# Feed-forward weights turned by VectorE in 32x32 blocks instead of by TensorE

## The reference, cut to what matters

```python
def _mx_dequant(t):                      # blocks of 32 along the last axis
    blocks = t.reshape(rows, feat // 32, 32)
    scales = jnp.maximum(jnp.max(jnp.abs(blocks), axis=-1) / 448.0, 1e-30)
    q = (blocks / scales[..., None]).astype(jnp.float8_e4m3fn).astype(jnp.float32)
    return (q * scales[..., None]).reshape(rows, feat)

x2d = layernorm(x)                                       # 1024 x 512
gate = _mx_dequant(x2d) @ _mx_dequant(gate_w).T          # gate_w, up_w: 2048 x 512
up   = _mx_dequant(x2d) @ _mx_dequant(up_w).T
h    = silu(gate) * up                                   # 1024 x 2048
x    = x + _mx_dequant(h) @ _mx_dequant(down_w).T        # down_w: 512 x 2048
```

## Time and profile before

| What | Before |
|---|---|
| Median of 3 runs | 1952.19 us (1952.12 to 1955.88) |
| Span of the profiled execution | 1951.1 us; the median of the runs is 1.1 us above it |
| PE busy | 1859.3 us, 95% |
| DVE busy | 1261.4 us, 65% |
| ACT busy | 698.1 us, 36% |
| POOL busy | 340.2 us, 17% |
| Mean granted TensorE clock | 0.985 |
| Weight transposes of the last stage (L2897, f_w) | 192 |
| First and last of them start | 1579.0 and 1877.6 us |

### The profile page before, as it was taken

The page is one execution under the profiler, slowest core; times in us unless marked ns, Lnnn a source line. Parts: engine busy times, 40 slices in busy tenths (PEclk is TensorE's granted clock), DMA queues, the critical chain, the costliest instruction groups (busy, mean ns, idle before and its releaser), DMA issues. The chain is left out here.

```text
span 1951.1 us, 24909 instructions
## 1 busy us (share of the span) xinstructions
PE 1859.3 (95%) x9496; PEld 1398.7 (72%) x9496; DVE 1261.4 (65%) x2133; ACT 698.1 (36%) x1123; POOL 340.2 (17%) x258
## 2 busy tenths in 40 slices
PE   7999999899999999999999999999989999999998
PEld 5777876444443578758888888888878875788886
DVE  5324755665761666686787687787762498866656
ACT  3302232345445478732342342333234331222211
POOL 0000010211200268711121111211210001212122
PEclk9999998999999899999999999999999999999999
DMA  6102222233321221132222213314212100110101
GB/s 217 44 0 71 87 71 55 50 74 74 93 50 46 85 66 66 44 123 88 77 78 101 97 58 111 105 39 133 76 35 76 65 25 19 65 44 24 42 1 44
DMA packets 69638, 132.58 MB, mean 68 GB/s; under 512 B 8960, under 2 KB 27392, under 8 KB 67984
## 3 DMA queue, kind: packets, MB, share of 16 engines
q1 hardware_dynamic: 69520, 130.99, 21.3%
HBM read 97.21 MB, written 14.75 MB: 57 GB/s over the span
## 5 line engine op out<-in xcount | busy, mean ns | idle before, releaser
L784 DVE TENSOR_REDUCE b_nm<-ps 128x1 f32<-128x1024 f32 x128 | 153.1, 1219 | 91.2 <-PE ps L772 91.2
L1270 ACT ACTIVATE b_pr<-ps 128x512 f32<-128x512 f32 x256 | 133.5, 603 | 135.6 <-PE ps L1182 135.4
L230 PE MATMUL ps<-d_x_high,d_w_high 128*128 128x512 f32 x384 | 154.6, 403 | 1.7 <-issue 1.7
L232 PE MATMUL ps<-d_x_high,d_w_low 128*128 128x512 f32 x384 | 150.0, 391 | 0.0
L231 PE MATMUL ps<-d_x_low,d_w_high 128*128 128x512 f32 x384 | 149.9, 390 | 0.0
L1194 PE MATMUL ps<-b_pr,b_VS 128*64 128x512 f32 x512 | 131.3, 637 | 0.0
L2229 POOL TENSOR_TENSOR d_sqsum<-d_sqsum,d_sq 128x512 f32<-128x512 f32 x32 | 45.4, 1422 | 468.4 <-ACT d_sq L2141 468.1
L1727 POOL TENSOR_TENSOR c_h<-c_h,c_w_row 128x512 f32<-128x512 f32 x64 | 105.7, 1657 | 50.4 <-DMA c_w_row<-w_rows 27.9
L1182 PEld LDWEIGHTS ps<-b_qS,b_kS 98*128 98x128 f32 x256 | 43.9, 193 | 78.5 <-issue 52.1
L1182 PE MATMUL ps<-b_qS,b_kS 98*128 98x512 f32 x256 | 93.1, 447 | 7.0 <-ACT b_pr L1270 3.5
L772 PE MATMUL ps<-b_kS,b_qS 96*128 96x512 f32 x256 | 82.6, 408 | 5.8 <-DVE b_nm L784 4.5
(11 more groups left out here) (439 smaller groups left out, 4971.0 us busy)
## 6 DMA issues: line engine op xcount, KB each, us to landing
b_kS<-b_k_parts SPq DMA_DIRECT2D x96, 128.0 KB, 2.3
f_rows<-d_fw SPq DMA_DIRECT2D x24, 512.0 KB, 3.8
f_w<-f_rows SPq DMA_DIRECT2D x12, 1024.0 KB, 4.8
c_w_row<-w_rows SPq DMA_DIRECT2D x16, 512.0 KB, 3.6
b_qS<-b_q_parts SPq DMA_DIRECT2D x96, 64.0 KB, 2.0
a_convT<-in_convT SPq DMA_DIRECT2D x4, 1024.0 KB, 12.8
d_w<-in_d_wq SPq DMA_DIRECT2D x16, 256.0 KB, 3.7
d_w<-in_d_wk SPq DMA_DIRECT2D x16, 256.0 KB, 2.8
```

The lines of the kernel that those rows point to most:

```text
L230: nc.tensor.matmul(out, lhsT[0], rhs[0], start=start, stop=False)
L232: return nc.tensor.matmul(out, lhsT[1], rhs[0], start=False, stop=stop)
L784: nc.vector.tensor_reduce(nm[:, g % 2, u:u + 1], c.ps[:, banks:banks + 2, :], AX.XY, ALU.max, negate=True).then_inc(job_read, 1)
L1270: nc.scalar.activation(pr[:, n % RING, :], c.ps[:, 4 + n % BANKS, :], ACT.Exp).then_inc(exp_done, 1)
```

## The change

The weight tiles are no longer turned by PE. DVE turns each in 32x32 blocks from `f_w` into one staging tile `wS` (128x512, a single buffer); ACT copies the staging tile as the high part; POOL subtracts to get the low part. DVE may turn the next tile only when POOL has done the low part of the one before.

Since DVE can only turn within a group of 32 partitions, the raw weights are loaded in another layout: each of the 48 tile loads becomes 4 DMAs, one for each group of 32 partitions, with runs of 128 features (512 bytes). With that the features come out in another order over the partitions, and the normalised x and h are written in the same order (`scale_by_blocks`, and `by_blocks` in the product of h).

```diff
-            sp.dma_start(fw[:, u % FSLOTS, i * BANK:(i + 1) * BANK], raw_rows(c, FR * u + i)).then_inc(in_f[u % FSLOTS], 16)
+            for b in range(P // MX):
+                sp.dma_start(fw[b * MX:(b + 1) * MX, u % FSLOTS, i * BANK:(i + 1) * BANK].rearrange("o (c f) -> o c f", f=P),
+                             raw_rows(c, FR * u + i, b)).then_inc(in_f[u % FSLOTS], 16)
...
+    def scale_by_blocks(self, dve, t):
+        nc.vector.tensor_scalar(by_blocks(c.xn[:, t, :]), in_order(c.x[:, t, :]), c.mv[:, t, 0:1], c.rstd[:, t:t + 1],
+                                ALU.subtract, ALU.mult).then_inc(self.normed, 1)
...
+    wS = c.at("f_wS", [P, KD, P], F32, 205.5)
...
-                    sp.wait_ge(turned, TURN_AT[("w", j - 2, KD - 1)] + 1)
+                    sp.wait_ge(w_turned, KD * (j - 1))
...
# GpSimd
+            def lows(units):
+                for i in units:
+                    pool.wait_ge(w_high_done, i + 1)
+                    high_, low_ = weight_parts(i)
+                    nc.gpsimd.tensor_tensor(low_, wS[:], high_.bitcast(F32), ALU.subtract).then_inc(w_low_done, 1)
+
+            lows(range(W_FIRST))
             for t in range(TT):
                 norm.root_pool(pool, t)
...
+            for s in range(STEPS + LAG):
+                early, middle, late = w_places(s) if s < STEPS else ([], [], [])
+                lows(early)
+                for u in ROUNDED_AT.get(s, []):
+                    products(XU + u)
+                lows(middle + late)
+                for u in SCALED_AT.get(s, []):
+                    ratios(XU + u)
...
# VectorE
+            def turn_weights(i):
+                dve.wait_ge(in_w[i // KD % 2], 16 * (i // KD // 2 + 1))
+                if i >= 1:
+                    dve.wait_ge(w_low_done, i)
+                nc.vector.transpose(wS[:].rearrange("p k (c o) -> p c k o", o=MX),
+                                    w[:, i // KD % 2, i % KD * DM:(i % KD + 1) * DM]
+                                    .rearrange("p (c k i) -> p c k i", k=KD, i=MX)).then_inc(w_turned, 1)
+
+            def weights_on(units, s):
+                for i in units:
+                    if i + 1 in w_turns(s):
+                        turn_weights(i + 1)
+
+            def weights_ahead(s):
+                if s < STEPS and w_turns(s):
+                    turn_weights(w_turns(s)[0])
...
             shift(NJ - 1)
+            turn_weights(0)
             for j, (b, m) in enumerate(JOBS):
...
-                low(TURNS[j])
+                if j + 1 < W_FIRST:
+                    turn_weights(j + 1)
...
-                for r in early:
-                    low(r)
+                weights_on(early, s)
                 for u in ROUNDED_AT.get(s, []):
                     unit_round(XU + u)
-                for r in middle:
-                    low(r)
+                weights_on(middle, s)
                 if s < STEPS:
...
-                    nc.vector.tensor_tensor(h[:, s % HR, :], c.ps[:, 4 + s % 2, :], silu[:, s % 2, :],
-                                            ALU.mult).then_inc(h_done, 1)
-                    for r in late:
-                        low(r)
+                    nc.vector.tensor_tensor(by_blocks(h[:, s % HR, :]), in_order(c.ps[:, 4 + s % 2, :]),
+                                            in_order(silu[:, s % 2, :]), ALU.mult).then_inc(h_done, 1)
+                    weights_on(late, s)
                     for u in SCALED_AT.get(s, []):
                         unit_scales(XU + u)
+                weights_ahead(s + 1)
...
# TensorE
-                turn(TURNS[j])
...
                     pe.wait_ge(low_done, TURN_AT[("x", t)] + 1)
-                    pe.wait_ge(low_done, TURN_AT[("w", 3 * n + 1, KD - 1)] + 1)
+                    pe.wait_ge(w_low_done, KD * (3 * n + 2))
                     up(s, 2 + s % 2, gT, silu_done, g_done)
-                    for r in middle:
-                        turn(r)
                     up(s, 4 + s % 2, uT, h_done, u_done)
-                    for r in late:
-                        turn(r)
...
# ScalarE
+            def high_turned(i):
+                act.wait_ge(w_turned, i + 1)
...
+                nc.scalar.activation(weight_parts(i)[0], wS[:], ACT.Copy).then_inc(w_high_done, 1)
...
-                high(TURNS[j])
+                high_turned(j)
...
-                    for r in early:
-                        high(r)
+                    for i in early:
+                        high_turned(i)
                     act.wait_ge(g_done, s + 1)
...
                     nc.scalar.activation(silu[:, s % 2, :], c.ps[:, 2 + s % 2, :], ACT.Silu).then_inc(silu_done, 1)
-                    for r in middle + late:
-                        high(r)
+                    for i in middle + late:
+                        high_turned(i)
```

More of the change, by code:

```diff
@@ L20, with raw_rows, by_blocks, in_order @@
 FJOBS = [(name, n) for n in range(4) for name in ("f_g", "f_u", "f_d")]
-def raw_rows(c, i):
+def raw_rows(c, i, b):
     name, n = FJOBS[i // KD]
-    rows = slice((i % KD) * P, (i % KD + 1) * P)
+    rows, cols = slice((i % KD) * P, (i % KD + 1) * P), slice(b * P, (b + 1) * P)
     if name == "f_d":
-        return c.dram[name][rows, n * BANK:(n + 1) * BANK]
-    return c.dram[name][n * BANK:(n + 1) * BANK, :][rows, :]
+        w = c.dram[name][:, n * BANK:(n + 1) * BANK]
+    else:
+        w = c.dram[name][n * BANK:(n + 1) * BANK, :]
+    return w[rows, cols].rearrange("(c o) f -> o c f", o=MX)
+def by_blocks(rows):
+    return rows.rearrange("p (k b i) -> p b k i", k=KD, i=MX)
+def in_order(rows):
+    return rows.rearrange("p (b k i) -> p b k i", k=KD, i=MX)
 class Core:
@@ L2634, in w_turns @@
         first = 0 if n == 0 else 2 * (t % 2)
-        return [("w", j, first + i) for i in range(count)] if 3 * n + 2 <= j < len(FJOBS) else []
+        return [KD * j + first + i for i in range(count)] if 3 * n + 2 <= j < len(FJOBS) else []
     def w_places(s):
@@ L2659, in mx_feed_forward @@
     FIRST = [("x", 0), ("x", 1)]
-    TURNS = [("w", j, r) for j in range(2) for r in range(KD)] + FIRST
+    TURNS = list(FIRST)
     for s in range(STEPS + LAG):
-        TURNS += x_turns(s) + h_turns(s) + (w_turns(s) if s < STEPS else [])
+        TURNS += x_turns(s) + h_turns(s)
     TURN_AT = {e: i for i, e in enumerate(TURNS)}
+    W_FIRST = 2 * KD
+    w_turned, w_high_done, w_low_done = (c.sem(f"f_{n}") for n in ("w_turned", "w_high_done", "w_low_done"))
     in_w = [c.sem(f"f_in_w{i}") for i in range(2)]
@@ L2712, in turn_parts, with weight_parts @@
         return [p_[:, e[1] % 2, :, :] for p_ in hF]
-    def bank_at(i):
-        return 4 + i % 2 if i < 2 * KD else i % 2
+    def weight_parts(i):
+        name, n = FJOBS[i // KD]
+        into = {"f_g": gT, "f_u": uT, "f_d": dT}[name]
+        return [p_[:, n % 2, :, i % KD * P:(i % KD + 1) * P] for p_ in into]
     def turn_bank(e):
-        return c.ps[:, bank_at(TURN_AT[e]), :].rearrange("p (k o) -> p k o", k=KD)
+        return c.ps[:, TURN_AT[e] % 2, :].rearrange("p (k o) -> p k o", k=KD)
     def e_tile(part, t):
@@ L2842, in _ @@
                 if t >= 1:
-                    norm.scale_dve(dve, t - 1)
+                    norm.scale_by_blocks(dve, t - 1)
                 if t == 2:
@@ L2896, in turn @@
                 for k in range(KD):
-                    last = nc.tensor.transpose(c.ps[:, bank_at(i), k * P:(k + 1) * P], turn_rows(e)[:, k * P:(k + 1) * P], c.ident[:])
+                    last = nc.tensor.transpose(c.ps[:, i % 2, k * P:(k + 1) * P], turn_rows(e)[:, k * P:(k + 1) * P], c.ident[:])
                 last.then_inc(turned, 1)
@@ L3013, in high @@
                 act.wait_ge(turned, TURN_AT[e] + 1)
-                if e[0] == "w" and e[2] == 0:
-                    name, n = FJOBS[e[1]]
+                if e[0] == "h" and e[1] >= 2:
+                    act.wait_ge(out_done, e[1] - 1)
+                nc.scalar.activation(turn_parts(e)[0], turn_bank(e), ACT.Copy).then_inc(high_done, 1)
+            def high_turned(i):
+                act.wait_ge(w_turned, i + 1)
+                if i % KD == 0:
+                    name, n = FJOBS[i // KD]
                     if name == "f_d" and n >= 2:
@@ L3020, in high @@
                         act.wait_ge(u_done, TT * (n - 1))
-                elif e[0] == "h" and e[1] >= 2:
-                    act.wait_ge(out_done, e[1] - 1)
-                nc.scalar.activation(turn_parts(e)[0], turn_bank(e), ACT.Copy).then_inc(high_done, 1)
+                nc.scalar.activation(weight_parts(i)[0], wS[:], ACT.Copy).then_inc(w_high_done, 1)
             def high_weights(i):
```

30 lines of the change are left out of this document (6 added, 24 removed).

## The result

The changed kernel takes 1960.15 us (median of 4 runs, 1958.47 to 1961.56), the kernel before beside it 1952.38 (4 runs, 1952.12 to 1955.88): ratio 1.0039, 95% interval 1.0027 to 1.0051. It is slower by 7.8 us, 0.4%. The profiled execution took 1959.69 us with a span of 1957.5, so 6.4 us more span than before.

What follows compares the result with a forecast made beforehand. PE was taken as the bound, except in the gate jobs and steps 0 to 8; 17.7 at step 8 + 1.6 clock - 12.3 for steps 10 to 27 = +7.0, span 1958.1, with 1.1 outside 1959.2 us; range 1951 to 1971.

Steps and rivals of the forecast that it cites:

- The turn on DVE: Every weight tile: one DVE turn takes 0.68 us, with bounds 0.42 and 1.22.
- The rivals with a cheap tile: Twelve tiles of steps 5 to 7: 1.80 us each gives 1948, chance 0.12; 2.23 each gives 1953, chance 0.12.
- Steps 10 to 27, -12.3: Later steps, PE the bound: 28 turns at 0.44 us removed gain 12.3 us; the 14 steps shrink to 8.65.
- The slack that I had worked out: Steps with two tiles: h's low part ends at 4.2 us, PE needs it at 5.9; slack 1.7, no wait.
- the fifth rival: Two-tile steps don't fit: a tile takes 3.7 us, no gain in steps 10 to 27, total 1983; chance 0.08.
- The chain of twelve, step 8 17.7 us late: Steps 5 to 8: twelve tiles 32.8 us plus 8.0 between them put step 8's gate product 17.7 us later.
- the 5.0 in step 6: Third tile of step 6: POOL's low part stands behind products, which wait for DVE's whole rounding; +5.0 us.
- The clock, +1.6: PE's restart in step 8 after its pause: a low granted clock costs 1.6 us, bounds 0 and 5.7.
- The gate jobs, -0.8: Gate jobs: 0.8 us gained, not 3.5, as the last numerators wait for DVE's products of z and gate.
- Linear attention, 0: Linear attention: 144 more DMAs on SP cost nothing, up to +9.6 us; the rival with that cost had chance 0.08.
- where I had 1.1: Time outside the span: 1.1 us, added to the forecast span of 1958.1.

Runs made afterwards that it cites:

- step 6 tiles first: Changed kernel with step 6's two middle tiles queued ahead of DVE's rounding and POOL's products: 1960.56 us, ratio to before 1.0044.
- PE kept busy: Changed kernel with 44 more PE products into an idle bank ahead of the wait of step 8: 1959.94 us, ratio to before 1.0038.
- the kernel with the loads alone: Kernel before with only the raw weight loads in the new layout, PE still turning the tiles: 1951.20 us, ratio to before 0.9993.
- the one with two staging tiles: Changed kernel with two staging tiles used in turn, all tiles still turned by DVE: 1947.03 us, ratio to before 0.9968.
- the kernel with PE on steps 5 and 6: Changed kernel with two staging tiles and PE turning the eight tiles of steps 5 and 6: 1944.89 us, ratio to before 0.9954.
- the last two experiments: Changed kernel with two staging tiles, PE turning the tiles of step 5 only (1943.02 us) or of steps 5 and 6 (1944.89 us).
- DVE's low parts: Changed kernel with the low parts of the first 20 tiles taken by DVE instead of POOL: 1957.44 us, ratio to before 1.0032.

## Why the prediction was right

Forecast 1959.2, measured 1960.15, by the mechanism forecast; that the two are so close is in part luck, as the end of this section shows. By the prediction's own steps:

- **The turn on DVE**: 0.68 taken, 0.698 measured. By the fixed term that the Trainium skill, VectorE: DVE Perf Modes, gives in its section on the TRN2 errata, my estimate had been 0.69; the trace agrees. With ACT's 0.63 and POOL's 1.28 and hand-overs a tile takes 2.82 (2.73 forecast). The Trainium skill, GPSIMD Engine Reference, section Performance versus the Vector engine, would have had the low part at 1.1 us (estimate); the measured 1.28 decides. The rivals with a cheap tile fall with it.
- **Steps 10 to 27, -12.3**: from the gate product of step 8 to the end TensorE's turns were worth 13.1 (252.9 against 239.8, two kernels with the chain out of the way). From the turn of h in step 10 to that in step 28 it is 12.5 (168.0 against 155.6). The other 0.6 lies behind the last turn of h, was not forecast, and its cause stays open. The slack that I had worked out held: no step of two tiles waits, and the fifth rival falls.
- **The chain of twelve, step 8 17.7 us late**: relative to the outputs 18.8 late (18.5 forecast). Its first turn came at 1674.31, 1.6 before 1675.9 as the outputs did; twelve tiles took 33.8 (32.8 forecast) and what stands between them 7.2 (8.0). PE stood 12.15 us ahead of step 6 and 13.44 ahead of step 8, where I had 12 and 16. My account of the 5.0 in step 6, though, had DVE's rounding in it only by way of POOL's order; the experiment that changed the order showed DVE's own work to hold the tiles up as long.
- **The clock, +1.6**: 2.3 (242.1 against 239.8), within its bounds.
- **The gate jobs, -0.8**: the step that was mis-sized, by its sign too. They took 2.3 us more: 0.6 for DVE's turn ahead of job 0, which came as forecast, and 1.7 from the first gF to the first sum of x, where I had 1.4 less. DVE's turn waited for POOL behind jobs 0, 3 and, which I had missed, 6. DVE and PE in order of time, and a window:

```profile
1604.51 7.94 PE L3016 MATMUL ps<-e_woT,e_gF 128*128 128x512 f32 x14 [0.78 <-DVE e_gF L2880]
...
1605.29 0.71 DVE L2801 STREAM_TRANSPOSE f_wS<-f_w 128x512 f32<-128x512 f32 x1 [0.81 <-POOL f_uT_low L2774]
...
1609.91 0.69 DVE L2885 TENSOR_TENSOR x<-ps,x 128x512 f32<-128x512 f32 x1 [2.62 <-PE ps L3016]
```

```profile
1604.00:1608.00 4.00, 3.49 (x5) 1.48 (x6) 2.45 (x4) 1.04 (x2) 2.44 (x2) 0.57 0.20 43
```

  PE had not waited for gF before; now it did four times, 3.1 us in all, and the granted clock fell to 0.57 behind the last of them. From the first output tile to its sum it took 5.4 us instead of 3.6. In two of the experiments with the same code (step 6 tiles first, PE kept busy) the clock did not fall there and the stretch was 30.7 and 30.6, with the same four waits of PE. So the waits alone use up what PE's turns gave, the turn ahead of job 0 adds its 0.6, and the clock adds 1.6 to 1.8.
- **Linear attention, 0**: shown by the kernel with the loads alone (535.6 us from the first to the last d_w_high in both, 535.8 after).
- **What the sum left out**: all that lies ahead of the gate jobs came 3.9 us earlier. 2.3 of it is there at the first d_w_high (831.5 before, 829.2 after), ahead of all that was changed; over the twelve profiled kernels this row lies between 828.1 and 831.8. The other 1.6 is at the end of the linear attention, where after is alone among the twelve (48.6 us from the last d_w_high to the last d_sq, the others 50.1 to 50.3). I take both for the spread of one execution. And 2.2 us lay outside the span after, where I had 1.1; over the experiments that part is 1.7 to 2.2, once 3.3, and what makes it up stays open.

So the errors of the sum (+3.1 in the gate jobs, +0.7 for the clock, +0.3 for the chain, -0.8 from step 8 on, -3.9 for the start, +1.1 outside) nearly cancelled, which is luck; the forecast was better than its terms.

## What to carry to other kernels

Work taken off the bounding engine is a gain only where that engine is the bound; where other work is crammed ahead of a first use, the path by other engines must be summed from its first possible start to that use, with each queue's own work in it. A staging buffer that is read by two engines in turn makes a serial chain of all three; ask for a second one before asking for faster instructions (13.4 us here). And a change may be split by place: the old way for the twelve crowded tiles, the new way for the rest, gave 10 us, and 15 with a second staging tile, where the whole change had cost 8. Such a split has a price of its own where it changes the loads: look for it ahead of the place that is being tested.

## What the runs showed of the hardware

Much of the spread of these kernels goes with TensorE's clock. The same two pauses ahead of the same products (1.60 and 0.98 us, around x's turns) were followed by the high clock in one execution and by the low in another. PE's turns of x in the kernel after and in the one with two staging tiles:

```profile
1648.39 1.09 PE L2938 MATMUL ps<-ident,xn 128*128 128x128 f32 x8 [1.60 <-DVE xn L2620]
1661.48 1.03 PE L2938 MATMUL ps<-ident,xn 128*128 128x128 f32 x8
```

```profile
1648.44 1.09 PE L2938 MATMUL ps<-ident,xn 128*128 128x128 f32 x8 [1.60 <-DVE xn L2620]
1664.41 1.04 PE L2938 MATMUL ps<-ident,xn 128*128 128x128 f32 x8
```

13.1 us between them in the first, 16.0 in the second, with the same instructions in it. Low windows of this kind stood there in four of the twelve profiled kernels; in the kernel with PE on steps 5 and 6:

```profile
1650.00:1655.00 5.00, 5.00 (x13) 3.84 (x13) 4.93 (x13) 0.00 (x0) 0.00 (x0) 0.50 0.01 2
```

The six executions of that kernel took 1939.1 and 1939.6 us with a mean granted clock of 0.986, and 1944.6 to 1945.8 with 0.982 or 0.983. What decides between the two I did not find; a median over few runs may fall in either group, so the 1.9 us between the last two experiments say nothing.

Beside a two-input instruction of POOL some of DVE's take longer: the two scalings at 1685.13 in the kernel after took 1.03 us beside POOL's low part, the same pair 0.29 at 1673.81, where POOL stood.

```profile
1673.81 0.29 DVE L2591 TENSOR_SCALAR f_scale<-f_scale 128x16 f32<-128x16 f32 x2
...
1685.13 1.03 DVE L2591 TENSOR_SCALAR f_scale<-f_scale 128x16 f32<-128x16 f32 x2
```

The length of a load's runs can cost time where its bytes stay the same. With 48 tiles in runs of 512 bytes DVE waited 3.3 us for them and the kernel lost nothing; with 20 of the tiles in runs of 128 bytes, the same bytes in all, it waited 6.3 us and the linear attention was 4.9 us longer, in one profiled execution. With twelve of them it was 0.9 longer, as much as in one kernel with runs of 512 bytes alone (DVE's low parts), so of the twelve nothing can be said.
